# Attention cores of layers 2 to 4: the order of score tiles, value tiles and maxima within a batch

## The reference

```
q_big  = einsum('bshk,hkq->bshq', q_hk, w_kc_q)           # 16 heads
q_r    = einsum('bshq,hqr->bhsr', q_big, W_qr)
k_r    = einsum('bld,hdr->bhlr', kv_rope, W_kr)
attn   = softmax(einsum('bhsr,bhlr->bhsl', q_r, k_r), axis=-1)
ctx_c  = einsum('bhsl,bld->bhsd', attn, kv_rope)
```

## Time and profile before

| | us |
|---|---|
| median of three runs | 2257.39 |
| lowest, highest | 2253.81, 2263.25 |
| the profiled execution, own time | 2262.48 |
| its span, first to last instruction | 2260.7 |
| PE busy | 2114.2 (94%) |
| DVE, POOL, ACT busy | 1476.9 (65%), 1407.9 (62%), 993.3 (44%) |

### The profile page before, as it was taken

One profiled execution on the slowest core, in us unless ns is written; L12 is line 12 of the kernel. 1 busy time (PEld: TensorE's weight loads), 2 busy tenths in 40 slices (PEclk: granted clock), 3 DMA queues, 4 the chain that ended last, 5 costly groups with the idle time before them and its releaser, 6 DMA issues.

```text
span 2260.7 us, 35590 instructions
## 1 busy us (share of the span) xinstructions
PE 2114.2 (94%) x13632; PEld 1465.0 (65%) x13636; DVE 1476.9 (65%) x2546; ACT 993.3 (44%) x1530; POOL 1407.9 (62%) x876
## 2 busy tenths in 40 slices
PE   7797999899999997897999999979997999999988
PEld 5586777656566564564665666568895665656588
DVE  6766863477777756666777777643334777777653
ACT  4452333355454445211544545434433544545443
POOL 0355763288878874454888888625441888888744
PEclk9898999999999998897999999989998999999989
DMA  3026875323223104002223222025433223222022
GB/s 93 30 86 181 252 252 154 73 69 69 56 59 79 42 29 132 24 1 60 56 55 75 63 56 65 19 71 156 140 86 73 56 55 71 67 55 62 10 67 79
DMA packets 65705, 179.60 MB, mean 79 GB/s; under 512 B 11280, under 2 KB 21280, under 8 KB 65154
## 3 DMA queue, kind: packets, MB, share of 16 engines
q1 hardware_dynamic: 65154, 177.01, 29.4%
q10 hardware_dynamic: 384, 0.33, 0.1%
HBM read 162.32 MB, written 14.98 MB: 78 GB/s over the span
## 4 chain that ended last, share of the span: by engine, by line
PE 80%; DVE 8%; POOL 4%; issue 3%; ACT 3%; DMA 1%; SPq 0%; ACTq 0%; POOLq 0%; DVEq 0%
PE psum L925 20%; PE psum L1453 20%; PE psum L1463 19%; PE psum L1381 7%; PE psum L1617 2%; PE psum L1480 2%; PE psum L1385 2%; PE psum L1574 2%; DVE mx L2439 1%; POOL CL L1916 1%; PE psum L1308 1%; PE psum L1186 1%; DMA bd<-in_blockdiag 1%; DVE mx L2423 1%; PE psum L1206 1%
## 5 line engine op out<-in xcount | busy, mean ns | idle before, releaser
L1894 ACT ACTIVATE E<-psum 125x896 f32<-125x896 f32 x576 | 519.9, 919 | 577.7 <-PE psum L1453 540.4
L2439 DVE TENSOR_REDUCE mx<-psum 128x1 f32<-128x500 f32 x945 | 561.8, 668 | 126.8 <-PE psum L1385 70.3
L2177 POOL TENSOR_TENSOR SA<-SA,E 125x896 f32<-125x896 f32 x282 | 595.5, 2112 | 69.4 <-ACT E L1894 50.8
L1463 PE MATMUL psum<-E,V 125*64 125x448 f32 x2304 | 472.3, 545 | 0.0
L1381 PE MATMUL psum<-KH,QH 64*128 64x500 f32 x864 | 331.6, 403 | 26.3 <-DVE mx L2423 24.0
L1463 PEld LDWEIGHTS psum<-E,V 125*64 125x64 f32 x2304 | 163.0, 136 | 233.3 <-issue 176.8
L1453 PE MATMUL psum<-QH,KH 64*125 64x448 f32 x1152 | 282.5, 414 | 2.4 <-ACT E L1894 2.4
L2177 POOL TENSOR_TENSOR SA<-SA,SB 125x896 f32<-125x896 f32 x93 | 194.2, 2088 | 124.8 <-DVE SB L2457 78.3
L1453 PE MATMUL psum<-QL,KH 64*125 64x448 f32 x1152 | 271.3, 364 | 0.0
L1453 PE MATMUL psum<-M,ones 64*125 64x448 f32 x1152 | 271.3, 363 | 0.0
L1453 PE MATMUL psum<-QH,KL 64*125 64x448 f32 x1152 | 243.0, 363 | 0.0
(11 more groups left out here) (303 smaller groups left out, 3946.2 us busy)
## 6 DMA issues: line engine op xcount, KB each, us to landing
KH<-kt_scratch SPq DMA_DIRECT2D x96, 375.0 KB, 5.2
KL<-kt_scratch SPq DMA_DIRECT2D x96, 375.0 KB, 6.7
EW<-in_f_w SPq DMA_DIRECT2D x64, 256.0 KB, 8.7
kt_scratch<-kt SPq DMA_DIRECT2D x16, 750.0 KB, 7.9
WS<-in_f_w SPq DMA_DIRECT2D x31, 384.0 KB, 4.6
GB<-gates_scratch SPq DMA_DIRECT2D x36, 224.0 KB, 3.7
slot_of_t<-slots_scratch SPq DMA_DIRECT2D x64, 112.0 KB, 4.5
WoT<-in_a_WoT SPq DMA_DIRECT2D x24, 256.0 KB, 4.0
```

Source lines behind the costliest of these rows:

```text
L1463: i = e.matmul(psum[c * DC:(c + 1) * DC, 4, 0:HT], V[0:LP, b, k * DC:(k + 1) * DC], E[g[n, b, k] % NE][0:LP, half[c]], start=k == 0, stop= ...
L1894: e.activation(E[m % NE][0:LP, :].rearrange("p (c q) -> p c q", c=2), psum[0:LP, pair:pair + 2, 0:HT], ACT.Exp).then_inc(exp_set.sem, 1)
L2177: e.tensor_tensor(SA[b % 2][0:LP, :], a[0:LP, :], x[0:LP, :], ALU.add).then_inc(sum_set.sem, 1)
L2439: e.tensor_reduce(mx[:, b % 2, j * 3 + c:j * 3 + c + 1], psum[:, bank, 0:CW], AX.X, ALU.max).then_inc(small_free.sem, 1)
```

## The change

In the order list: one phase of twelve score tiles and then one of twelve value tiles in each batch. The three ends stand first. The 18 other maxima come in couples, both ahead of `head`, in front of tiles 1, 2, 3, 5, 6, 7, 9, 10 and 11. `evict` follows the batch's own last value tile, `total` of the batch before stands after value tile 2, `max_spread` after value tile 7, `add` of tiles 10 and 11 and then `div` of the batch before after value tile 8. Twelve E tiles instead of eight. The paired tiles are 8 and 9, 10 and 11; POOL adds nine times, as before. In the last batch of a layer `total` has three terms instead of four.

```diff
-PAIRED = {3: (2, 3), 9: (8, 9)}
+PAIRED = {9: (8, 9), 11: (10, 11)}
-ADDED = (1, 3, 4, 5, 6, 7, 9, 10, 11)
+ADDED = (1, 2, 3, 4, 5, 6, 7, 9, 11)
...
     for b in range(B):
+        sides = [(t, c) for t in range(3) for c in range(3)] if b + 1 < B else []
         if b + 2 < B:
             order.append(("load_keys", b + 2))
         if b + 1 < B:
             order.append(("load_lows", b + 1))
...
+            order += [("max", b + 1, 3, c) for c in range(3)]
+        for k in range(NL):
+            if sides and k % 4:
+                t, c = sides.pop(0)
+                order += [("max", b + 1, t, c), ("max", b + 1, t + 4, c)]
+            order += [("head", b, k), ("scores", b, k)]
+            if k == 4 and b + 1 < B:
+                order.append(("low", b + 1))
+        order += [("max_total", b + 1)] if b + 1 < B else []
+        order.append(("add", b, 9))
+        for k in range(NL):
+            order.append(("values", b, k))
+            if k == 1 and b + 2 < B:
+                order += [("high", b + 2), ("diag", b + 2)]
+            if k == 2 and b > 0:
+                order.append(("total", b - 1))
+            if k == 7 and b + 1 < B:
+                order.append(("max_spread", b + 1))
+            if k == 8:
+                order.append(("add", b, 11))
+                order += [("div", b - 1)] if b > 0 else []
+                order += [("total", b)] if b == B - 1 else []
+        order.append(("evict", b) if b + 1 < B else ("div", b))
+    return order
...
-    NE = 8
-    E = [mem.take("E", [P, T], F32) for _ in range(NE - 1)]
+    NE = 12
+    E = [mem.take("E", [P, T], F32) for _ in range(NE - 5)]
...
-    E.append(mem.take("E", [P, T], F32))
+    E += [mem.take("E", [P, T], F32) for _ in range(3)]
...
     SB = [mem.take("SB", [P, T], F32) for _ in range(2)]
+    E += [mem.take("E", [P, T], F32) for _ in range(2)]
...
-                if (j, c) == (0, 0):
+                if (j, c) == (3, 0):
...
-                    e.wait_ge(*pair_set.at(n, b, 9))
-                    e.wait_ge(*exp_set.at(n, b, NL - 1))
-                    terms += [SB[1], E[g[n, b, 10] % NE], E[g[n, b, 11] % NE]]
+                    e.wait_ge(*pair_set.at(n, b, NL - 1))
+                    terms += SB
```

More of the change, by code:

```diff
@@ L283, in core_order @@
     order += [("max_total", 0), ("max_spread", 0)] + makes[7:] + [("diag", 1)]
-    ends = [(j, c) for j in (3,) for c in range(3)]
-    sides = [(t + 4 * odd, c) for t in range(3) for c in range(3) for odd in range(2)]
     for b in range(B):
+        sides = [(t, c) for t in range(3) for c in range(3)] if b + 1 < B else []
         if b + 2 < B:
@@ L290, in core_order @@
             order.append(("load_lows", b + 1))
[L291 to L318, removed]
@@ L319, in core_order @@
-    return order + [("values", B - 1, NL - 1), ("div", B - 1)]
+            order += [("max", b + 1, 3, c) for c in range(3)]
[7 more added lines that the diff above has]
+        order += [("max_total", b + 1)] if b + 1 < B else []
@@ L530, in build @@
     SB = [mem.take("SB", [P, T], F32) for _ in range(2)]
+    E += [mem.take("E", [P, T], F32) for _ in range(2)]
+    assert mem.at <= yh_end
     at(top)
```

## The result

Median of 20 runs after: 2250.04 us (2245.63 to 2255.72); of 20 runs before beside them: 2257.19 us (2249.07 to 2263.25). The ratio is 0.997, 95% interval 0.9959 to 0.998: 7 us faster. The forecast was 2261, no faster than before. The profiled executions have spans of 2260.7 before and 2253.9 after, both at a mean granted clock of 0.963.

The account below looks back on a forecast made before the run. PE's queue set the 24.55 us batch; after, POOL with DVE would at 24.6, with PE's 11.24 + 13.08 = 24.32 inside. With layer ends, +1.1 a layer, +3.3 in all: 2261 us beside the 2257.39 median, range 2233 to 2288.

Parts of the forecast that it names:

- Edges: PE's phase changes in a batch: one values-to-scores, one scores-to-values and the `evict` wait go, 0.52 us a batch.
- (c): PE's wait for `evict` before the value tile after `total`: 0.17 us a batch, to go.
- (a): PE's edge from values to scores: 0.20 us, one a batch to go.
- (b): PE's edge from scores to values: 0.15 us, one a batch to go.
- Score phase 13.08: PE's twelve score tiles with 18 maxima: 13.08 us against 12.78 before, held by DVE's return of three banks.
- The lock: POOL and DVE exclude each other when both read two SBUF tiles; DVE's add was to lengthen POOL's queue by 0.95.
- POOL with DVE sets the batch at 24.6: Closed ring from next batch's first reduction through POOL's additions to `div`: 3.70 + 20.9 = 24.6 us, above PE's 24.32.
- Ends of a layer: First and last batches counted apart: layer sum 393.7 us against 392.6, +1.1 a layer, +3.3 in all.
- The lock does not bite: Rival: DVE's adds slip in without lengthening POOL's, PE's 24.32 a batch holds: 2249 us, chance 0.15.
- The couples pay in full: Rival: maxima banks come back before asked for, score phase 12.3, 1.0 us a batch saved: 2212 us, chance 0.10.
- `div` behind POOL: Rival: `div` waits a whole POOL addition, 2.2 us a batch: 2360 us, chance 0.07; part of it 2279, 0.17.
- Slow spacing: Rival: DVE's reductions start 0.67 apart, not 0.586; phase 13.57, batch 24.8: 2270 us, chance 0.03.

Follow-up runs that it names:

- the half reductions with POOL relieved: Kernel after, DVE reducing 250 of 500 columns and POOL adding 448 of 896: 2214.76 us, ratio 0.98, batch 23.58.
- The relieved POOL: Kernel after, each POOL addition over 448 of 896 columns: 2248.52 us, ratio 0.9955, batch 24.35.
- the tenth addition: Kernel after, POOL adding tiles 8 and 9 one by one instead of DVE pairing them: 2304.33 us, ratio 1.0194, batch 25.39.
- the spread order: Kernel after, 18 maxima spread, none to two ahead of each `head`: 2231.13 us, ratio 0.9866; with eight POOL additions 2229.12 us, 0.986.

## Why the prediction was wrong, point by point

- **Edges, 0.52 a batch: right, as far as shown.** (c) is measured gone, alone worth 0.20 where 0.17 was said. (a) and (b), 0.35 together, are only argued one by one; the sum of PE's batch bears them out.
- **Score phase 13.08: right**, 13.1 measured. The same steps carried to the exponentials space them by 1.19, 1.17, 1.17 and 0.90; the trace has 1.21, 1.17, 1.16 and, inside the pair, 0.93. The hand-over of 0.82 from DVE to PE, assumed like ACT's, holds to a few hundredths. Of the waits foretold for tiles 2, 3, 6 and 7 the weight loader's records show those of 2 and 3. The cause, banks returned by DVE every 0.586, is shown by the half reductions with POOL relieved: 12.34.
- **PE's own batch, 24.32: right**, 24.35 where DVE is in time.
- **The lock: right in kind.** Adds of 2.2 us on DVE, POOL's three additions of 7.14 instead of 6.53, and 1.08 for DVE's as soon as POOL's are short. The Trainium skill (SBUF — State Buffer, SBUF: two separate sides) has this as an exclusive lock, and this trace agrees, with 2.25 against 1.08.
- **"POOL with DVE sets the batch at 24.6": wrong, and the step that failed.** The closed ring measures 24.24, just inside PE's 24.35. The part from POOL's first addition to the end of `div` was put at 20.9; it measured 20.6 (521.39 to 541.98). Three terms were too large. DVE's `add` in between lengthens POOL by 0.74 (three additions take 7.22 from the first's start to the next step's, 6.48 undisturbed), not 0.95. QL takes 1.11 from its start to the next addition's (530.07 to 531.18), not 1.19. And the addition that ends the sum was counted at the 2.17 between two starts, where its record is 2.10. The last 0.08 is that the reduction starts before `div`'s record ends. The 0.95 is how long after POOL's operation DVE's `add` ends, which it is here too (541.44 after 540.50); I took it as the whole delay of POOL's next addition, and that is less. 0.28 was all that lay between the ring and PE's sum, so an error of 0.36 turned the forecast, and I gave the ring no bounds. The relieved POOL shows that the ring does not set the batch after; the tenth addition and the longer batch show that it stands within 0.1 to 0.15 of doing so.
- **The sign for the lock: too coarse.** "A batch of 24.3 would make the lock wrong", the prediction said. The batch is 24.35, and the records show the lock in every batch. A period can't tell a lock that is absent from one that is covered.
- **Ends of a layer: nearly.** From M of batch 0 to the end of the last RS a layer went by -1.9, -2.6 and -1.9 us. With PE's 24.32 for the thirteen batches that it has at 24.6, the sum gives -2.5; the first batch, put at 24.1, took 23.6. The last batch lost some 0.4: its two reciprocals start 7.15 apart, 6.77 with POOL's additions halved. The `add` that `total` waits for and then `div` of batch 14 stood behind POOL:

```profile
825.03 2.96 DVE L2456 RECIPROCAL RS<-psum 128x448 f32<-128x448 f32 x1 [2.90 <-PE psum L1475]
827.91 1.47 DVE L2452 TENSOR_TENSOR SB<-E,E 125x896 f32<-125x896 f32 x1
829.30 2.77 DVE L2461 TENSOR_TENSOR QR<-OB,RS 128x448 f32<-128x448 f32 x1
832.18 2.96 DVE L2456 RECIPROCAL RS<-psum 128x448 f32<-128x448 f32 x1
```

  The three layers together make -6.4 of the -6.8 between the spans.
- **The rivals.** "The lock does not bite" had the time, 2249, and not the mechanism: the lock bites and is covered, and its number was right by luck. "The couples pay in full" would need the banks free; the short reductions give such a phase (12.34), and the spread order comes near it (23.78 less 11.24 is 12.54 with eight additions). "`div` behind POOL" occurs only at layer ends, and with a tenth addition in every batch. "Slow spacing" has nothing for it: reductions start 0.586 apart here too. The section of the Trainium skill that the prediction names for it (VectorE: DVE Perf Modes, The DRAIN you can't avoid) also says that a next operation that is not held starts earlier, and this trace agrees, with 0.586 beside records of 0.67.

So why did a large change give so little? It took 0.52 out of a batch in edges and put 0.3 back by crowding 18 maxima into nine tiles on three banks. What is left is 0.2, as much as the edge at `evict` brings by itself.

## What to carry to other kernels

Where two loops through different engines come within 2% of each other, give each its own error and test which one sets the period by relieving one at a time; relieving both gives the floor. A buffer ring that an engine returns at a fixed rate wants its users evenly spaced: the same 18 matmuls were worth 0.53 us a batch by their places alone. Before merging phases, do the edge that costs a wait by itself; it may be the whole gain.

## What the runs showed of the hardware

- A reduction of 500 columns from PSUM has a record of 0.67 and starts 0.586 after the one before; with 250 columns five take 1.79, 0.36 each. A reduction that only waits for `div` on DVE starts 0.08 before the end of its record. Neither length of reduction is stretched by POOL's additions, and the subtraction M, with one operand in PSUM, keeps 0.69.
- DVE's two-operand add of 125x896 took 1.08 beside short POOL additions, up to 3.0 beside whole ones, by how much of POOL's was still to run: it ends 0.94 to 0.96 after it. POOL's lengthening by it (0.74) is less than DVE's (1.1 with an add of 2.2, 1.9 with one of 3.0).
- The length of an add's record on DVE is no measure of cost: its mean went from 1.23 to 2.20 and the kernel got faster, because the add was asked for early and nothing behind it was due.
